# State-space stage of a four-layer block: the next group's six convolution tiles, one or two to a step over four steps

## The reference, cut to what matters

```python
proj = jnp.einsum('bld,pd->blp', hidden_states, in_proj_w)
gate, hbc, dt = proj[..., :I], proj[..., I:I + CONV_DIM], proj[..., -H:]
pad = jnp.pad(hbc, ((0, 0), (K - 1, 0), (0, 0)))
conv = conv_bias
for k in range(K):                                   # K = 4 taps
    conv = conv + pad[:, k:k + L, :] * conv_weight[:, k]
xBC = jax.nn.silu(conv)                              # x, B and C of the scan
...
state = state * dA_t[..., None, None] + dtx_t[..., None] * B_t[:, :, None, :]
y_t = jnp.einsum('bhpn,bhn->bhp', state, C_t)
...
yn = (yg * lax.rsqrt(var + EPS)).reshape(B, L, I) * norm_weight
yn = yn * jax.nn.silu(gate)
out = jnp.einsum('bli,di->bld', yn, out_proj_w)
```

## Time and profile before

| | |
|---|---|
| median of 3 runs | 1824.86 us (1823.95 to 1825.76) |
| the profiled execution | 1824.79 us, its span 1823.0 us |
| mean granted TensorE clock | 0.939 of full |
| PE busy | 1573.8 us (86%), 8870 instructions |
| DVE busy | 1392.2 us (76%) |
| POOL busy | 1026.2 us (56%) |
| ACT busy | 760.7 us (42%) |
| chain that ended last | PE 58%, DVE 25%, issue 7%, POOL 4%, ACT 4%; PE's line 350 alone 31% |

### The profile page before, as it was taken

The page is one execution under the profiler, slowest core; times in us unless marked ns, Lnnn a source line. Parts: engine busy times, 40 slices in busy tenths (PEclk is TensorE's granted clock), DMA queues, the critical chain, the costliest instruction groups (busy, mean ns, idle before and its releaser), DMA issues.

```text
span 1823.0 us, 26503 instructions
## 1 busy us (share of the span) xinstructions
PE 1573.8 (86%) x8870; PEld 1231.1 (68%) x8870; DVE 1392.2 (76%) x2223; ACT 760.7 (42%) x1390; POOL 1026.2 (56%) x861
## 2 busy tenths in 40 slices
PE   3788999989989999899899869997589999988791
PEld 2577777767777777687677647885357676666581
DVE  5578998989989989989999875556537776768525
ACT  2344444434443434344344213332136766664131
POOL 3267777677678676866876864003433443327544
PEclk9899999999999999999999888998689999998696
DMA  3111011021021110110211021122000000041344
GB/s 112 35 36 63 19 47 58 12 69 35 12 74 35 46 58 17 66 37 12 75 35 33 27 64 58 69 69 92 1 1 13 1 13 1 1 160 72 104 139 161
DMA packets 49496, 92.59 MB, mean 51 GB/s; under 512 B 8016, under 2 KB 32720, under 8 KB 44176
## 3 DMA queue, kind: packets, MB, share of 16 engines
q1 hardware_dynamic: 45744, 79.58, 13.4%
q0 software_dynamic: 3680, 12.06, 2.0%
HBM read 81.14 MB, written 10.49 MB: 50 GB/s over the span
## 4 chain that ended last, share of the span: by engine, by line
PE 58%; DVE 25%; issue 7%; POOL 4%; ACT 4%; DMA 1%; SPq 0%; DVEq 0%; POOLq 0%; ACTq 0%
PE banks L350 31%; PE banks L1723 6%; DVE tap L1191 3%; PE banks L1842 3%; PE banks L1733 2%; PE banks L1801 2%; DVE y L1276 2%; PE banks L1832 2%; PE banks L1616 2%; DVE em L1306 2%; DVE wcl L355 2%; PE banks L1656 2%; DVE ynTl L355 1%; DVE acc L618 1%; PE banks L1647 1%
## 5 line engine op out<-in xcount | busy, mean ns | idle before, releaser
L1191 DVE SCALAR_TENSOR_TENSOR tap<-banks,parg,tap 128x511 f32<-128x511 f32 (+2 forms) x288 | 214.8, 746 | 23.9 <-ACT tap L918 17.1
L700 POOL TENSOR_TENSOR am<-ah,upto 128x1024 fp32r<-128x1024 f32 x64 | 129.6, 2026 | 161.1 <-PE banks L1616 121.4
L350 PE MATMUL banks<-xTh,wch 128*128 128x512 f32 x384 | 170.7, 444 | 23.0 <-DVE sg L1245 22.9
L853 POOL TENSOR_SCALAR kz<-kst,head 128x512 fp32r<-128x512 f32 x64 | 99.1, 1567 | 159.9 <-DVE kst L1420 159.9
L1306 DVE TENSOR_TENSOR em<-em,gmask 128x1024 f32<-128x1024 f32 x64 | 141.9, 2217 | 21.6 <-ACT em L970 21.1
L350 PE MATMUL banks<-xTh,wcl 128*128 128x512 f32 x384 | 155.4, 405 | 0.0
L350 PE MATMUL banks<-xTl,wch 128*128 128x512 f32 x384 | 155.0, 404 | 0.0
L926 ACT ACTIVATE th<-tap 128x512 f32<-128x512 f32 x96 | 60.8, 633 | 218.5 <-DVE tap L1191 215.6
L700 POOL TENSOR_TENSOR am<-al,upto 128x1024 fp32r<-128x1024 f32 x64 | 149.1, 2330 | 0.0
L1123 ACT ACTIVATE prob<-banks,nmax 128x128 f32<-128x128 f32 (+3 forms) x256 | 121.9, 530 | 54.3 <-DVE nmax L1436 54.1
L1436 DVE TENSOR_REDUCE nmax<-banks 128x2 f32<-128x256 f32 (+3 forms) x128 | 104.8, 819 | 39.8 <-PE banks L1833 39.7
(11 more groups left out here) (290 smaller groups left out, 4571.6 us busy)
## 6 DMA issues: line engine op xcount, KB each, us to landing
x<-grownT SPq DMA_DIRECT2D x96, 128.0 KB, 4.7
x<-in_w_conv SPq DMA_DIRECT2D x7, 1536.0 KB, 6.7
x<-in_w_gate SPq DMA_DIRECT2D x8, 1024.0 KB, 4.8
x<-in_w_out SPq DMA_DIRECT2D x8, 1024.0 KB, 4.8
eraw<-in_expert_w SPq DMA_DIRECT2D x8, 1024.0 KB, 7.7
gur<-in_ff_gu SPq DMA_DIRECT2D x7, 1024.0 KB, 4.7
x<-in_hidden SPq DMA_DIRECT2D x16, 256.0 KB, 3.8
mates<-yd SPq DMA_DIRECT2D x8, 512.0 KB, 4.3
```

The lines of the kernel that those rows point to most:

```text
L350: m = nc.tensor.matmul(o, a, b, start=first and n == 0, stop=last and n == len(terms) - 1)
L700: m = pool.tensor_tensor(am[:, part, :, :], a[:, i, :].bitcast(F32).unsqueeze(2).to_broadcast([P, HG, P]), upto[:, :].unsqueeze(1).to_broa ...
L853: m = pool.tensor_scalar(kz[:, quad % 2, p2, j, :], kst[:, p2, :].bitcast(F32), head[:, j:j + 1], None, ALU.mult)
L1191: nc.vector.scalar_tensor_tensor(tap[:, q % 2, sh:L], bk(CONV_BANKS[q % 2])[:, 0:L - sh], parg[:, KC * q + k:KC * q + k + 1], tap[:, q % 2 ...
```

## The change

Steps 4 to 7 of every group but the last make 1, 2, 2 and 1 tiles of the next group in place of 2, 2, 2 and 0. The first tile of a step uses bank 0 and the second bank 2, whichever number it has; the half of `tap` still goes by the tile's number. What only a second tile needs is asked for by the count of tiles.

```diff
-            if s in (4, 5, 6) and not last:
-                return (NB * CT + 2 * (s - 4), NB * CT + 2 * (s - 4) + 1)
+            if s >= 4 and s < NT and not last:
+                return tuple(NB * CT + q for q in ((0,), (1, 2), (3, 4), (5,))[s - 4])
...
-            def first_tap(n, q):
+            def first_tap(n, q, bank):
...
-                nc.scalar.activation(tap[:, q % 2, :], bk(CONV_BANKS[q % 2]), ACT.Identity,
+                nc.scalar.activation(tap[:, q % 2, :], bk(bank), ACT.Identity,
...
                 if tiles:
-                    first_tap(n0 + tiles[0], tiles[0] % CT)
+                    first_tap(n0 + tiles[0], tiles[0] % CT, CONV_BANKS[0])
                     tanh(n0 + tiles[0], tiles[0] % CT)
...
-                if tiles:
-                    first_tap(n0 + tiles[1], tiles[1] % CT)
+                if len(tiles) > 1:
+                    first_tap(n0 + tiles[1], tiles[1] % CT, CONV_BANKS[1])
...
                     silu(n0 + tiles[0], tiles[0] % CT, tiles[0] // CT % NB)
-                    convolve(n0 + tiles[1], tiles[1] % CT)
+                if len(tiles) > 1:
+                    convolve(n0 + tiles[1], tiles[1] % CT, CONV_BANKS[1])
...
-                if tiles:
+                if len(tiles) > 1:
                     pe.wait_ge(e_ready, NT * g + s + 1)
-                    convolved(n0 + tiles[1], tiles[1] % CT, tiles[1] // CT % NB)
+                    convolved(n0 + tiles[1], tiles[1] % CT, tiles[1] // CT % NB, CONV_BANKS[1])
```

More of the change, by code:

```diff
@@ L1017, in _ @@
             act.wait_ge(par_ready, 1)
-            first_tap(0, 0)
+            first_tap(0, 0, CONV_BANKS[0])
             act.wait_ge(dve_step, 3)
@@ L1024, in _ @@
             nc.scalar.activation(z[:, 1, :], z[:, 2, :], ACT.Ln, bias=1.0).then_inc(dt_act, 1)
-            first_tap(1, 1)
+            first_tap(1, 1, CONV_BANKS[1])
             tanh(0, 0)
@@ L1036, in _ @@
                 if q + 1 < CT:
-                    first_tap(q + 1, q + 1)
+                    first_tap(q + 1, q + 1, CONV_BANKS[(q + 1) % 2])
                 tanh(q, q)
@@ L1182, in decays_of, with convolve @@
                 low(nc.vector, al[:, :, :], a, ah[:, :, :]).then_inc(ah_ready, 1)
-            def convolve(n, q):
+            def convolve(n, q, bank):
                 dve.wait_ge(tap0, n + 1)
@@ L1190, in convolve @@
                         dve.wait_ge(taps, 3 * n + sh - 1)
-                    nc.vector.scalar_tensor_tensor(tap[:, q % 2, sh:L], bk(CONV_BANKS[q % 2])[:, 0:L - sh],
+                    nc.vector.scalar_tensor_tensor(tap[:, q % 2, sh:L], bk(bank)[:, 0:L - sh],
                                                    parg[:, KC * q + k:KC * q + k + 1],
@@ L1223, in _ @@
             chain(nc.vector.scalar_tensor_tensor(z[:, 1, :], z[:, 0, :], -1.0, z[:, 0, :], ALU.mult, ALU.min))
-            convolve(0, 0)
+            convolve(0, 0, CONV_BANKS[0])
             dve.wait_ge(dt_act, 3)
@@ L1236, in _ @@
             decays_of(0)
-            convolve(1, 1)
+            convolve(1, 1, CONV_BANKS[1])
             silu(0, 0, 0)
@@ L1249, in _ @@
                 if q + 1 < CT:
-                    convolve(q + 1, q + 1)
+                    convolve(q + 1, q + 1, CONV_BANKS[(q + 1) % 2])
                 silu(q, q, 0)
@@ L1310, in step @@
                 if tiles:
-                    convolve(n0 + tiles[0], tiles[0] % CT)
+                    convolve(n0 + tiles[0], tiles[0] % CT, CONV_BANKS[0])
                 if making:
@@ L1577, in _, with convolved @@
             pe.wait_ge(wdt_lo, 1)
-            def convolved(n, q, b):
+            def convolved(n, q, b, bank):
                 ch, tok = slice(q * P, (q + 1) * P), slice(b * L, (b + 1) * L)
-                products(bk(CONV_BANKS[q % 2]), [(wch[:, k, ch], wcl[:, k, ch], xTh[:, k, tok], xTl[:, k, tok])
+                products(bk(bank), [(wch[:, k, ch], wcl[:, k, ch], xTh[:, k, tok], xTl[:, k, tok])
                                                  for k in range(KT)]).then_inc(h_ready, 1)
@@ L1624, in step @@
                     pe.wait_ge(gate_used, NT * g + s + 3)
-                    convolved(n0 + tiles[0], tiles[0] % CT, tiles[0] // CT % NB)
+                    convolved(n0 + tiles[0], tiles[0] % CT, tiles[0] // CT % NB, CONV_BANKS[0])
                 if not (first and s < 2):
@@ L1683, in _ @@
             pe.wait_ge(wc_lo, KT)
-            convolved(0, 0, 0)
+            convolved(0, 0, 0, CONV_BANKS[0])
             pe.wait_ge(dt_t, 2)
@@ L1688, in _ @@
             m.then_inc(dt_tr, 1)
-            convolved(1, 1, 0)
+            convolved(1, 1, 0, CONV_BANKS[1])
             pe.wait_ge(dve_step, 9)
@@ L1698, in _ @@
                 pe.wait_ge(taps, 3 * (q - 1))
-                convolved(q, q, 0)
+                convolved(q, q, 0, CONV_BANKS[q % 2])
                 if q == 3:
```

## The result

The changed kernel takes 1850.33 us (median of 4 runs, 1848.08 to 1852.92) against 1825.31 us for the one before (4 runs), a ratio of 1.0138 with a 95% interval of 1.0120 to 1.0156: 25.0 us slower. The forecast was 1856 us, 31 us slower, with a range of 1840 to 1868. The profiled execution took 1850.7 us, its span is 1849.0 us, 26 more than before, and the mean granted clock 0.937 (0.935 to 0.939 in the four; before 0.939).

What follows compares the result with a forecast made beforehand. PE was taken to bound the kernel, through its waits and clock. Per group +4.0 - 0.6 - 0.4 = +3.0 us, x 7 = +21, plus 10 for the clock: 1824.8 us becomes 1856 us, range 1840 to 1868.

Steps and rivals of the forecast that it cites:

- What bounds: Whole kernel: PE, busy 86% of the span; only its waits and its clock can be won or lost.
- Step 4, -0.6 us: Without its second tile, step 4 ends only 0.6 us sooner; the gate waits 2.1 us for the first tile's taps.
- The lower bound: Step 4's saving at least 0.3 us, because a product after a wait takes up to 0.4 us longer.
- Step 7, +4.0 us: With a first tile added, step 7 grows 4.0 us, bounds +1.4 and +6.0; PE waits ahead of state's product and gate.
- Point (b): Step 7: DVE's mask precedes the state's read and begins when POOL's instruction ends; state's product waits 1.2 us, not 1.46.
- Step 0, -0.4 us: Next group's step 0 loses its 0.38 us wait for the first tile's taps; bounds 0 and -0.4.
- The clock, +10 us: Half-clock stretches behind PE's new waits in steps 4 and 7: 7 x 1.4 = +10 us, bounds 0 and 22.
- the 14 places: New idle places of PE, two in each group, in steps 4 and 7; half were counted as halving the clock.
- the rival with the clock untouched: Steps 4 and 7 wait as forecast without half-clock stretches: 1846 us, 1841 to 1849; chance 0.22.
- The sum: Whole kernel: +21 us at an unchanged clock and +10 us for the clock, 1856 us.
- The faster case: The tile fills PE's idle time in step 7 and step 4 gives back all 2.88 us: 1812 us; chance 0.05.
- Step 7 costs half as much: The mask is let in between POOL's instructions, taps start earlier, step 7 grows by 2.4 us: 1835 us; chance 0.10.

Runs made afterwards that it cites:

- waits_filled: Changed kernel, with products that nothing reads put into PE's new waits in steps 4 and 7: 1839.79 us, ratio 1.0072.
- before_decays_later: Kernel before (2, 2, 2, 0 tiles), with DVE making the next group's decays behind the low part of y in step 7: 1815.00 us, ratio 0.9948.
- late_place: Changed kernel, with step 4's single tile in the second place (bank 2) and ACT waiting for the parameters only ahead of its first tap: 1829.33 us.
- read_first: Changed kernel, with DVE reading the state's part ahead of the mask in step 7, as before the change: 1863.07 us, ratio 1.0202.
- two_two_one_one: Steps 4 to 7 make 2, 2, 1, 1 tiles, so against the changed kernel step 7's tile comes from step 6: 1830.01 us, ratio 1.0020.
- decays_later: Changed kernel (1, 2, 2, 1 tiles), with DVE making the next group's decays behind the low part of y in step 7: 1841.47 us, ratio 1.0089.
- late_place_and_decays: Changed kernel with the edits of late_place and decays_later together: 1818.40 us, ratio 0.9965.
- both_late: late_place_and_decays, with step 7's single tile in the second place (bank 2) too: 1815.73 us, ratio 0.9952.
- before_filled: before_decays_later, with 13 products that nothing reads in PE's 3.25 us wait at the head of step 4: 1805.30 us, ratio 0.9893.

## Why the prediction was right

- **What bounds.** Right. Steps 5 and 6 are 14.9 and 16.0 us in both kernels; the difference lies in the steps with PE's waits, and in its clock.
- **Step 4, -0.6 us.** Right in mechanism and nearly in size: the gate's wait for the taps is 2.15 us (worked out as 2.1), and with the clock kept full behind it in waits_filled the step is 19.65 us against 20.15. The lower bound rested on a wrong reading: the 0.80 us product stands behind no wait in its row, and is as long in before_decays_later, where PE doesn't wait; products behind a wait took 0.50. late_place shows the other half: with the tile out of bank 0 the wait is gone.
- **Step 7, +4.0 us.** Measured 3.95 at full clock; waits of 1.33 and 1.04 us where 1.2 and 1.2 to 1.7 were worked out; the gate's products started at 594.90, 10.2 us into the step, forecast 10.3. Point (b), that the mask's work begins when POOL's instruction ends, held in read_first (the mask ends 1.07 us after POOL's scaling of the state) and, for POOL's first half of `am`, in two_two_one_one. What I missed in it: the blocking hangs on who starts first, here by 0.24 us. In decays_later the mask started 0.07 us ahead, and it was POOL that took longer. Compared like with like, though, the tile's price in step 7 is the same: with POOL first 15.87 against 11.93 us, 3.95 more, and with DVE first 14.53 (decays_later) against 10.46 (before_decays_later), 4.07 more. The order is a cost beside it, 1.35 to 1.46 us of step 7 in either kernel, and the kernel before paid it too.
- **Step 0, -0.4 us.** Right in sign, mis-sized: 0.68 us, and 0.2 more in step 1; together 6.1 us over the groups in place of 2.8. The 0.38 us wait is gone as forecast; what the other 0.3 us and step 1's 0.2 are, no run takes apart.
- **The clock, +10 us.** Half of the 14 places were counted. The clock fell behind eight of them, four in step 7 and four in step 4, but in two of the latter (groups 4 and 6) it had stayed full at the head of the step, so six stretches were added (and one of twice the length, in group 5, is single). That is 6.0 us in step 7 and about 3.2 in step 4; filling all 14 places gave 10.5 us. The cause is shown, the count of seven was a guess that came out. The row of the 1.86 us wait pointed the right way, and by luck: in the changed kernel the same wait stands there with the clock full behind it.

```profile
1061.06 0.38 PE L1633 MATMUL banks<-ones,ysq 128*128 128x1 f32 x2 [1.86 <-POOL ysq L718]
```

```profile
1061.10:1064.50 3.40, 2.42 (x20) 1.40 (x20) 3.33 (x11) 0.61 (x2) 3.40 (x2) 1.00 0.00 0
```

By the page "TensorE: Matmul & The Clock Gate" of the Trainium skill, section "Why this matters for your kernels", which warns of longer idle gaps only, the rival with the clock untouched was due. The trace does not agree: waits of 2.15 and 2.55 us and pairs of 1.33 and 1.04 us were followed by the half clock.

- **The sum**, 31 us against 25 (26 in the spans). The mis-sized term is steps 0 and 1, -6.1 us for -2.8. Of the rest, step 4 gave 0.7 us less than forecast, step 7 and the clock cost 0.3 and 0.8 us less, and the sum lacked a term: outside groups 0 to 6 the span fell by another 1.2 us, where group 7's half-clock stretches landed elsewhere.
- **The rivals.** The faster case needed both waits gone; both were there. "Step 7 costs half as much" was the right thing to fear, since the mask can be let in sooner: with DVE first step 7 is 14.5 us. But that comes of an order of two instructions that was already there before, and moving them shortens the kernel before as well.

Open: why a wait of the same length is followed by the half clock in one group and not in the next. The runs show that this is so, not what decides.

## What to carry to other kernels

When a piece of work is taken out of a queue, ask what it covered: here the next products waited for a semaphore that the piece had hidden, and 2.9 us of work gave back 0.5. Where two engines get in each other's way, look at which of them starts first, and by how little: moving two instructions of 0.2 us behind a longer one took 1.4 us out of step 7, of which step 0 took 0.5 back in the kernel before and nothing in the changed one. No spread of the tiles beat the kernel before without that move. Judge a change against a kernel with the same order: set against the kernel before as it stood, the tile seemed to cost 2.6 us with DVE first, and it cost 4.1. And count waits of TensorE twice, once for themselves and once for the clock behind them.

## What the runs showed of the hardware

- DVE and POOL, with operands in the local memory, ran one after the other and not side by side: the low part of y took 0.68 us when it started first and 2.21 us when POOL had started 0.24 us before; the mask 1.22 us unhindered and up to 2.91, ending 1.08 us after POOL's instruction did; POOL's half of `am` 1.90 us alone and 2.90 when the mask was first. DVE's taps, which read an accumulator bank, took 2.31 us whatever POOL did.
- Whether the half clock followed a wait did not go by its length alone. Behind waits of 2.04 to 2.15 us ahead of step 4's gate it came in 2 of 5 groups of the changed kernel, and in 7 of 7 of decays_later and of read_first; behind the 2.55 us wait in 2 of 2. Behind the wait of 3.3 us at the head of step 4 it came in 7 of 7 groups of the kernel before and in 5 of 7 of the changed one. Behind a head wait of 2.74 to 2.86 us it came in 7 of 7 of late_place_and_decays and in 1 of 7 of both_late; behind a 2.73 us wait in step 7 in 7 of 7 of read_first; behind a single wait of 1.03 us in none of the 14 of two_two_one_one.
- A half-clock stretch cost 1.3 to 1.6 us in steps 4 and 7, 1.1 more where it lasted twice as long, and 0.7 us in step 0 of both_late, where a wait of 0.55 us vanished behind it.
- Products that nothing reads, put into the waits of waits_filled and before_filled, left no half-clock stretch behind them and cost nothing that the times show: step 7 is 15.86 us with them and 15.87 without at the full clock.
